# Graph network on one core: the last graph masked and added by VectorE, z stored from ScalarE's queue, the start reordered

## The chip, the cores and the metric

The kernel runs on one core of a Trainium2 chip. Its engines are TensorE (PE: matmuls, with its weight loads as PEld), VectorE (DVE), ScalarE (ACT), GpSimd (POOL) and SyncE (SP), which here only issues DMAs. Each engine runs its own instructions in order; they meet through semaphores. The metric is the device time of one execution in microseconds (us).

## The reference

For each of 16 graphs, x is 512 nodes by 128 features and adj is 512 by 512.

```
h = x                                     # five layers, one GRU cell for all
for l in range(5):
    m   = h @ weight[l]
    agg = (adj != 0)^T @ m
    gi = agg @ w_ih.T + b_ih ;  gh = h @ w_hh.T + b_hh
    r = sigmoid(i_r + h_r); z = sigmoid(i_z + h_z); n = tanh(i_n + r * h_n)
    h = (1 - z) * n + z * h
y = layernorm(x + h * nodemask)
# second network: five groups g of the first 25 nodes, two normalised graph convolutions each
z = layernorm(y + sum_g softmax(fusion_w)[g] * conv(relu(conv(y[idx_g]))))   # rows 0..24; the others get z = layernorm(y)
```

## The kernel before

**The steps.** The 16 graphs times 5 layers are 80 steps k, in an order fixed by the table ROUNDS: graphs 0, 1, 2, 3 in their first layer are steps 0 to 3, then layers of several graphs take turns. State and messages are held transposed, features on the 128 partitions and the 512 nodes along the free axis. Every fp32 operand of a product is split into two fp16 halves (hi and lo), so a product is three matmuls: hi by hi, hi by lo, lo by hi (`split_product`).

**One step.** PE does `aggregate(k)` (8 matmuls over the adjacency held in fp8 as tile A8), `gates_of_state(k)` (9 matmuls of the weights WH by the state into the PSUM banks pHN, pR, pZ) and `gates_of_messages(k)` (9 matmuls of the merged weights WC by the messages AG into pR, pZ, pIN). ACT makes the hi half of the messages (`aggregated_hi`) and the sigmoids and the tanh. DVE makes the lo half (`aggregated_lo`), `candidate(k)` (two operations on tile T) and `new_state(k)` (two operations, the second writes H). POOL makes z*h (`kept_share`, tile ZH) and the lo half of the new state. PE may write pIN of step k only when H of step k-1 is there.

**Loads and transposes.** The adjacency of a graph (1 MB, fp32) is loaded into one of three slots of tile AS and cast to fp8 by DVE in two halves (`cast_half`; graph 0 in four quarters, `cast_first`). In a graph's first layer, its x in natural layout is split by ACT (`natural_hi`) and POOL (`natural_lo`) into tile NAT. From step 2 on, SP issues one DMA transpose per step: in a first layer it turns NAT into the state HT and waits for `natural_lo`; in a later layer it turns HT into NAT, for the aggregation of that step. SP's queue is in order, so a late transpose delays the next. `first_state` (POOL) sums the halves of a new graph's state.

**The start.** PE transposes x of graph 0, w_hh, w_ih and weight[0] (`L834` to `L839`). ACT copies the last two to SBUF (semaphore wi_v) and PE multiplies them (`merge(0, pIN)`), which gives the weights WC of layer 0; ACT and DVE split them (`merged_hi`, `merged_lo`). Then come the state products of step 0 into pHN and pR, the bias rows' transpose and `aggregate(0)` (`first_messages`), then pZ. Nothing here is scheduled by a tool: the order is the order in which the code of each engine is written.

**The end.** The three last steps also carry the tail of the second network: `conv_s` and `conv_d` of PE with copies on ACT between them, and five chained additions `fused` on DVE into tile FU, then the statistics of z (`stats_z`), POOL's power for the inverse root, and `normalise_z` into ZO. For the last graphs, PE transposes H back into PSUM (`back`), the node mask is multiplied on (`masked`, into YM), POOL adds x (`residual`, into Y), DVE makes statistics (`stats`), POOL the inverse roots, DVE the scaled means (`scales`), and ACT and DVE normalise. SP stores each graph in two DMAs (`store_y`, `L387` and `L388`) and z in one (`store_z`, `L393`).

Of the kernel before, what the change touches and what calls it, by code (L numbers as in the profile page):

```python
# [6 lines left out]
ALU = mybir.AluOpType  # L7
# [7 lines left out]
P = 128  # L15
B, N, D = 16, 512, 128
L = 5
NI = N // P
# [7 lines left out]
S = P // Q  # L26
# [88 lines left out]
def graph_net_kernel(nc, x, adj, nodemask, weight, w_ih, w_hh, b_ih, b_hh, W1, b1, W2, b2, fusion_w, out):  # L115
    ctx = ExitStack()
    with ctx:
# [226 lines left out]
        def _(sp):  # L344
# [79 lines left out]
            for b in range(B - 4, B):  # L424
                store_y(b)
            store_z(TAIL)
            for slot in range(4):
# [5 lines left out]
        def _(pool):  # L433
# [192 lines left out]
            normalise(E0, range(2))  # L626
            residual(B - 1)
            inverse_root(B - 2)
# [4 lines left out]
        def _(pe):  # L633
# [39 lines left out]
            def gates_of_state(k, between=lambda: None):  # L673
# [14 lines left out]
                if k > 0:  # L688
                    pe.wait_ge(sig_z, k)
                split_product(pZ, WH[:, 0, 1, :], WH[:, 1, 1, :], ht[0], ht[1], True, False)  # L690

            def gates_of_messages(k, between=lambda: None):
# [83 lines left out]

            def conv_s(groups, bank):
                for j, g in enumerate(groups):
                    for h in range(NH):
                        last = mm(bank[:, j * P:(j + 1) * P], H1[:, h, g, :], W2S[:, g, h, :],  # L780
                                  start=(h == 0), stop=(h == NH - 1))
                last.then_inc(c_mm, 1)

# [41 lines left out]
            def first_messages():  # L825
                pe.wait_ge(ld_r, 16 * 4)
                rows = ROWS.shape[0]
                tr(pC[:, 0:rows], ROWS[:, :], IDF[0:rows, 0:rows]).then_inc(cols_t, 1)
                aggregate(0)

# [8 lines left out]
            tr(pIN[:, 3 * D:4 * D], WL[:, 0, :], IDF[:, :]).then_inc(wi_t, 1)  # L839
            pe.wait_ge(wi_v, 1)  # L840
            merge(0, pIN)
            pe.wait_ge(wh_lo, 1)
            gates_of_state(0, first_messages)
            pe.wait_ge(x_lo, 1)
            transpose_x(1, pF)
# [38 lines left out]
            pe.wait_ge(c_ea, 5 * TAIL + 3)  # L884
            conv_s(range(0, 3), LAST_BANKS[3])
            back(B - 1)
            conv_s(range(3, G), LAST_BANKS[4])
# [6 lines left out]
        def _(act):  # L894
# [155 lines left out]
            natural_hi(1)  # L1050
            load_a(3)
            aggregated_hi(0)
            transposed_hi(1, pF)
            act.wait_ge(cols_v, 1)
            reset_gate(0)
            update_gate(0)
            new_gate(0)
            aggregated_hi(1)
# [45 lines left out]
            normalise(E0, range(2, NI))  # L1104
            masked(B - 1)
            for part, groups in enumerate(LAST_PARTS):
# [5 lines left out]
            normalise(B - 2)  # L1112
            normalise(B - 1, range(2, NI))

        @block.vector
        def _(dve):
# [134 lines left out]
            def normalise(b, blocks):  # L1251
# [4 lines left out]
                last.then_inc(f_dv, 1)  # L1256

            def softmax_shift():
                dve.wait_ge(ld_f, 16)
                link(v.tensor_reduce(FS[:, 1:2], FW[:, :], AX_X, ALU.max))  # L1260
                v.tensor_scalar(FX[:, :], FW[:, :], FS[:, 1:2], None, ALU.subtract).then_inc(fw_x, 1)
# [104 lines left out]
            cast_first(1)  # L1366
            merged_lo(0, pIN)
            cast_first(2)
            cast_first(3)
            dve.wait_ge(cols_t, 1)  # L1370
            link(v.tensor_copy(COLS[:, :], pC[:, 0:COLS.shape[1]]))
# [8 lines left out]
            for k in range(1, K):  # L1380
                if k == 2:
                    cast_half(3, 0)
                new_state(k - 1)
# [18 lines left out]
                for b in range(B):  # L1402
                    if b >= 4 and k == CAST_AT[b] + 1:
                        cast_half(b, 1)
                    if k == FINAL[b] + TURNED[b] + 2 and b < BY_DMA:
                        variances(b)
                candidate(k)
                if k <= 2:
                    aggregated_lo(k + 1)
# [42 lines left out]
            stats(B - 2)  # L1452
            fused(TAIL, range(0, 3))
            stats(B - 1)
            scales(B - 2)
            fused(TAIL, range(3, G))
            stats_z(TAIL)
# [25 lines left out]
```

## Time and profile before

| What | us |
|---|---|
| median of 3 runs | 511.0 (510.79 to 512.11) |
| the profiled execution, whole | 511.83 |
| its span, first to last event | 510.0 |
| PE busy | 492.1 (96%) |
| DVE busy | 382.4 (75%) |
| POOL busy | 311.1 (61%) |
| ACT busy | 300.9 (59%) |

The profiled execution lies 0.83 us above the median, and 1.8 us of its time lie outside its span. PE's granted clock is full (1.00) in every stretch up to 502 us. PE is busy in nearly every slice of the span except the first and the last, so the two ends, some 30 us at the start and some 15 us at the end, are where something else than PE's own work sets the time.

### The profile page before, as it was taken

What the parts mean: (1) busy time and instruction counts of PE and PEld (TensorE: products, weight loads), DVE (VectorE), ACT (ScalarE), POOL (GpSimd) and SP (SyncE); (2) the same over time, 40 slices, a digit from 0 to 9 for tenths busy, and PEclk for the clock granted to TensorE, in tenths of its full rate; (3) what the DMA queues carried; (4) which work ended last, traced back from release to release, by engine and by line L of the source; (5) the groups of instructions that cost most, each with busy time, mean ns of one, the idle gap of its engine ahead of it and who ended that gap; (6) DMA issues with size and microseconds to landing.
All of it is one profiled execution on the core that took longest, in us unless ns stands there. A gap on an engine that the chain in (4) does not pass through costs nothing.

```text
span 510.0 us, 7334 instructions
## 1 busy us (share of the span) xinstructions
PE 492.1 (96%) x2393; PEld 240.3 (47%) x2393; DVE 382.4 (75%) x727; ACT 300.9 (59%) x549; POOL 311.1 (61%) x282
## 2 busy tenths in 40 slices
PE   8999999999999999999999999999999999999992
PEld 5344444444444444444555444445544444564462
DVE  3777876687867788997677889876567878556794
ACT  4546655655656566666656665566565556754564
POOL 3654775757775688775777458766444645424564
PEclk9999999999999999999999999999999999999998
DMA  8768253654626446337826466242143251222212
GB/s 266 231 153 174 48 150 60 185 159 105 134 41 166 107 100 166 83 81 148 195 48 145 123 185 168 61 85 41 22 101 62 59 98 41 62 60 62 59 32 83
DMA packets 131610, 55.45 MB, mean 109 GB/s; under 512 B 95140, under 2 KB 123252, under 8 KB 131572
## 3 DMA queue, kind: packets, MB, share of 16 engines
q1 hardware_dynamic: 106336, 31.93, 30.4%
q10 hardware_dynamic: 25236, 23.05, 14.8%
q8 instruction: 19, 0.31, 0.2%
q14 instruction: 19, 0.16, 0.1%
HBM read 27.70 MB, written 4.19 MB: 63 GB/s over the span
## 4 chain that ended last, share of the span: by engine, by line
PE 77%; DVE 14%; ACT 4%; issue 3%; DMA 1%; ACTq 0%; DVEq 0%
PE pA L664 22%; PE pR L671 5%; PE pR L670 5%; PE pR L669 5%; PE pZ L669 5%; PE pZ L671 5%; PE pZ L670 5%; PE pIN L669 3%; PE pIN L671 3%; PE pIN L670 3%; PE pHN L669 3%; PE pHN L671 3%; PE pHN L670 3%; DVE T L1155 2%; DVE T L1159 2%
## 5 line engine op out<-in xcount | busy, mean ns | idle before, releaser
L484 POOL TENSOR_TENSOR HT<-H,HT 128x512 f16<-128x512 f32 x74 | 89.1, 1204 | 109.5 <-ACT HT L959 109.3
L664 PE MATMUL pA<-A,NAT 128*128 128x512 fp8e4 x640 | 151.2, 379 | 0.2 <-DVE A L1144 0.2
L473 POOL TENSOR_TENSOR ZH<-Z,H 128x512 f32<-128x512 f32 x80 | 102.5, 1281 | 38.7 <-ACT Z L972 37.0
L1155 DVE SCALAR_TENSOR_TENSOR T<-pHN,BHN,R 128x512 f32<-128x512 f32 x80 | 59.9, 748 | 74.8 <-ACT R L965 74.4
L976 ACT ACTIVATE pIN<-T,COLS 128x512 f32<-128x512 f32 x80 | 55.4, 692 | 76.5 <-DVE T L1159 76.4
L664 PEld LDWEIGHTS pA<-A,NAT 128*128 128x128 f16 x640 | 62.5, 98 | 72.1 <-DVE A L1144 0.7
L959 ACT ACTIVATE HT<-H 128x512 f16<-128x512 f32 x74 | 46.7, 631 | 64.3 <-DVE H L1168 64.3
L965 ACT ACTIVATE R<-pR,BRZ 128x512 f32<-128x512 f32 x80 | 54.5, 681 | 26.7 <-PE pR L671 26.5
L1164 DVE SCALAR_TENSOR_TENSOR pIN<-Z,pIN 128x512 f32<-128x512 f32 x80 | 55.1, 689 | 18.8 <-ACT pIN L976 18.7
L1150 DVE TENSOR_TENSOR AG<-pA,AG 128x512 f16<-128x512 f32 x80 | 54.7, 684 | 9.0 <-ACT AG L955 8.8
L955 ACT ACTIVATE AG<-pA 128x512 f16<-128x512 f32 x80 | 47.2, 590 | 20.6 <-PE pA L664 17.8
L1168 DVE TENSOR_TENSOR H<-ZH,pIN 128x512 f32<-128x512 f32 x80 | 54.9, 687 | 3.7 <-POOL ZH L473 1.0
L1159 DVE TENSOR_TENSOR T<-pIN,T 128x512 f32<-128x512 f32 x80 | 55.3, 691 | 3.0 <-PE pIN L671 0.2
L972 ACT ACTIVATE Z<-pZ,BRZ 128x512 f32<-128x512 f32 x80 | 54.7, 684 | 0.0
L669 PE MATMUL pIN<-AG,WC 128*128 128x512 f16 x80 | 30.4, 380 | 3.1 <-DVE H L1168 2.9
L669 PE MATMUL pHN<-HT,WH 128*128 128x512 f16 x80 | 30.4, 380 | 1.1 <-DVE T L1155 0.7
L669 PE MATMUL pR<-AG,WC 128*128 128x512 f16 x80 | 30.3, 379 | 0.8 <-DVE AG L1150 0.8
L670 PE MATMUL pHN<-HT,WH 128*128 128x512 f16 x80 | 30.3, 379 | 0.0
L671 PE MATMUL pHN<-HT,WH 128*128 128x512 f16 x80 | 30.3, 379 | 0.0
L669 PE MATMUL pR<-HT,WH 128*128 128x512 f16 x80 | 30.3, 379 | 0.0
L670 PE MATMUL pR<-HT,WH 128*128 128x512 f16 x80 | 30.3, 379 | 0.0
L671 PE MATMUL pR<-HT,WH 128*128 128x512 f16 x80 | 30.3, 379 | 0.0
(217 smaller groups left out, 845.0 us busy)
## 6 DMA issues: line engine op xcount, KB each, us to landing
AS<-in_adj_dram ACTq DMA_DIRECT2D x13, 1024.0 KB, 6.0
XR<-in_x_dram ACTq DMA_DIRECT2D x16, 256.0 KB, 3.0
XS<-in_x_dram ACTq DMA_DIRECT2D x13, 256.0 KB, 3.2
out_dram<-Y SPq DMA_DIRECT2D x16, 192.0 KB, 2.1
AS<-in_adj_dram SPq DMA_DIRECT2D x2, 1024.0 KB, 10.4
AS<-in_adj_dram SPq DMA_DIRECT2D x4, 256.0 KB, 5.4
NAT<-HT SPq DMA_TRANSPOSE x64, 3.1
XS<-in_x_dram SPq DMA_DIRECT2D x3, 256.0 KB, 8.4
```

The costliest lines, as they stand in the source:

```text
L473: g_.tensor_tensor(ZH[:, :], Z[:, :], H[:, b, :], ALU.mult).then_inc(zh_p, 1)
L484: g_.tensor_tensor(HT[:, b, 1, :], H[:, b, :], HT[:, b, 0, :], ALU.subtract).then_inc(h_lo, 1)
L664: last = mm(pA2[:, k % 2, :], NAT[:, k % 2, h, i, :], A8[:, b, i, :], start=(h == 0 and i == 0), stop=(h == 1 and i == NI - 1))
L669: mm(bank[:, :], w_hi, v_hi, start=start, stop=False)
L670: mm(bank[:, :], w_hi, v_lo, start=False, stop=False)
L671: return mm(bank[:, :], w_lo, v_hi, start=False, stop=stop)
L972: fn(Z[:, :], pZ[:, :], ACT.Sigmoid, bias=BRZ[:, 1:2], scale=UNSCALE).then_inc(sig_z, 1)
L976: fn(pIN[:, :], T[:, :], ACT.Tanh, bias=BI[:, 2:3], scale=UNSCALE).then_inc(n_a, 1)
L1155: v.scalar_tensor_tensor(out=T[:, :], in0=pHN[:, :], scalar=BHN[:, 0:1], in1=R[:, :], op0=ALU.add, op1=ALU.mult).then_inc(t_v, 1)
L1159: v.tensor_tensor(T[:, :], pIN[:, :], T[:, :], ALU.add).then_inc(u_v, 1)
L1164: v.scalar_tensor_tensor(out=pIN[:, :], in0=Z[:, :], scalar=1.0, in1=pIN[:, :], op0=ALU.subtract, op1=ALU.mult).then_inc(e_v, 1)
L1168: v.tensor_tensor(H[:, GRAPH[k], :], ZH[:, :], pIN[:, :], ALU.subtract).then_inc(h_v, 1)
```

## The change

At the start, PE does the first six state products (pHN and pR of step 0) before `merge(0)`, in an order that takes the hi by hi products first, and `merge(0)` moves into `first_messages`, behind the transpose of the bias rows and ahead of `aggregate(0)`. DVE does all four casts of graph 0 before `merged_lo(0)`. ACT issues the load of graph 3's adjacency after `update_gate(0)`, no longer right after `natural_hi(1)`. DVE's first half cast of graph 3 moves from between `aggregated_lo(2)` and `new_state(1)` to behind `candidate(1)`, ahead of `aggregated_lo(2)`.

At the end, the last graph (15) is masked and added by DVE in one operation per block of 128 nodes, read straight from PSUM (`masked_residual`); ACT's `masked(15)` and POOL's `residual(15)` go. PE transposes graph 15 back behind the first group of `conv_s` instead of behind the third. DVE does that graph's statistics and `scales(14)` ahead of all five `fused` additions. The last z is stored by ACT's queue, no longer by SP's.

```diff
 sync:    for b in range(B - 4, B): store_y(b)
-            store_z(TAIL)
 gpsimd:  residual(B - 2); normalise(E0, range(2))
-            residual(B - 1)
 tensor:
+            def first_gates_of_state():
+                hi, lo = HT[:, 0, 0, :], HT[:, 0, 1, :]
+                banks = [(pHN, 2), (pR, 0)]
+                pe.wait_ge(x_hi, 1)
+                pe.wait_ge(wh_hi, 1)
+                for bank, g in banks:
+                    mm(bank[:, :], WH[:, 0, g, :], hi, start=True, stop=False)
+                pe.wait_ge(x_lo, 1)
+                for bank, g in banks:
+                    mm(bank[:, :], WH[:, 0, g, :], lo, start=False, stop=False)
+                pe.wait_ge(wh_lo, 1)
+                for bank, g in banks:
+                    mm(bank[:, :], WH[:, 1, g, :], hi, start=False, stop=(bank is pHN))
+                first_messages()
+                split_product(pZ, WH[:, 0, 1, :], WH[:, 1, 1, :], hi, lo, True, False)
 ...
                 tr(pC[:, 0:rows], ROWS[:, :], IDF[0:rows, 0:rows]).then_inc(cols_t, 1)
+                pe.wait_ge(wi_v, 1)
+                merge(0, pIN)
                 aggregate(0)
 ...
-            pe.wait_ge(wi_v, 1)
-            merge(0, pIN)
-            pe.wait_ge(wh_lo, 1)
-            gates_of_state(0, first_messages)
-            pe.wait_ge(x_lo, 1)
+            first_gates_of_state()
             transpose_x(1, pF)
 ...
-            conv_s(range(0, 3), LAST_BANKS[3])
-            back(B - 1)
+            conv_s(range(0, 3), LAST_BANKS[3], lambda: back(B - 1))   # called after the first group
             conv_s(range(3, G), LAST_BANKS[4])
 scalar:
             natural_hi(1)
-            load_a(3)
 ...
             update_gate(0)
+            load_a(3)
             new_gate(0)
 ...
-            masked(B - 1)
 ...
             normalise(B - 1, range(2, NI))
+            act.wait_ge(z_o, NC)
+            act.dma_start(out[E0:B, 0:S, :], ZO[:, TAIL % 2, :]).then_inc(st_z[TAIL % 2], 16)
 vector:
+            def masked_residual(b):
+                dve.wait_ge(f_mm, b - BY_DMA + 1)
+                dve.wait_ge(st_y[b % 4], 32 * (b // 4))
+                dve.wait_ge(ld_xr[b % 3], 16 * (b // 3 + 1))
+                for i in range(NI):
+                    last = v.scalar_tensor_tensor(out=Y[:, b % 4, i, :], in0=BACK_BANKS[b][:, i * P:(i + 1) * P],
+                                                  scalar=MASK[:, b, i:i + 1], in1=XR[:, b % 3, i, :],
+                                                  op0=ALU.mult, op1=ALU.add)
+                last.then_inc(f_y, 1)
 ...
             cast_first(0)
             cast_first(1)
-            merged_lo(0, pIN)
             cast_first(2)
             cast_first(3)
+            merged_lo(0, pIN)
 ...
-                if k == 2:
-                    cast_half(3, 0)            # ahead of new_state(1)
 ...
                 candidate(k)
+                if k == 1:
+                    cast_half(3, 0)            # ahead of aggregated_lo(2)
 ...
             stats(B - 2)
-            fused(TAIL, range(0, 3))
+            masked_residual(B - 1)
             stats(B - 1)
             scales(B - 2)
+            fused(TAIL, range(0, 3))
             fused(TAIL, range(3, G))
```

PE at the start, before: the merge (into pIN, from tile BD, which holds the weights' scratch) stands ahead of the state products.

```order
L839 MATMUL pIN<-IDF,BD 128x128
L648 MATMUL pIN<-BD 128x384
L669 MATMUL pHN<-HT,WH 128x512
L670 MATMUL pHN<-HT,WH 128x512
L671 MATMUL pHN<-HT,WH 128x512
L669 MATMUL pR<-HT,WH 128x512
L670 MATMUL pR<-HT,WH 128x512
L671 MATMUL pR<-HT,WH 128x512
L828 MATMUL pC<-IDF,ROWS 128x80
L664 MATMUL pA<-A,NAT 128x512 x8
```

PE at the same place now; L697, L700 and L703 are the lines of the new function, L646 is the merge.

```order
L858 MATMUL pIN<-IDF,BD 128x128
L697 MATMUL pHN<-HT,WH 128x512
L697 MATMUL pR<-HT,WH 128x512
L700 MATMUL pHN<-HT,WH 128x512
L700 MATMUL pR<-HT,WH 128x512
L703 MATMUL pHN<-HT,WH 128x512
L703 MATMUL pR<-HT,WH 128x512
L845 MATMUL pC<-IDF,ROWS 128x80
L646 MATMUL pIN<-BD 128x384
L662 MATMUL pA<-A,NAT 128x512 x8
```

The merge went from directly behind the transposes of the weights to directly ahead of the first aggregation, with the six state products and the bias rows' transpose in between.

DVE at the end, before, from `scales` of graphs 12 and 13 on (FU is the sum of z, ST, MV and VE the statistics, NB the scaled means).

```order
L1242 SCALAR_TENSOR_TENSOR NB<-MV,RS 128x4 x2
L1220 BN_STATS ST<-Y 128x6 x4
L1227 BN_AGGR MV<-ST 128x2 x4
L1230 TENSOR_SCALAR VE<-MV 128x4
L1231 TENSOR_SCALAR VE<-MV 128x1
L1336 SCALAR_TENSOR_TENSOR FU<-pR,X 128x128
L1336 SCALAR_TENSOR_TENSOR FU<-pR,FU 128x128 x2
L1220 BN_STATS ST<-Y 128x6 x4
L1227 BN_AGGR MV<-ST 128x2 x4
L1230 TENSOR_SCALAR VE<-MV 128x4
L1231 TENSOR_SCALAR VE<-MV 128x1
L1242 SCALAR_TENSOR_TENSOR NB<-MV,RS 128x4
```

DVE at the same place now; L1278 is the new operation on graph 15.

```order
L1257 SCALAR_TENSOR_TENSOR NB<-MV,RS 128x4 x2
L1235 BN_STATS ST<-Y 128x6 x4
L1242 BN_AGGR MV<-ST 128x2 x4
L1245 TENSOR_SCALAR VE<-MV 128x4
L1246 TENSOR_SCALAR VE<-MV 128x1
L1278 SCALAR_TENSOR_TENSOR Y<-pHN,COLS,XR 128x128 x4
L1235 BN_STATS ST<-Y 128x6 x4
L1242 BN_AGGR MV<-ST 128x2 x4
L1245 TENSOR_SCALAR VE<-MV 128x4
L1246 TENSOR_SCALAR VE<-MV 128x1
L1257 SCALAR_TENSOR_TENSOR NB<-MV,RS 128x4
L1361 SCALAR_TENSOR_TENSOR FU<-pR,X 128x128
```

Four operations came in, and the first three additions into FU went behind graph 15's statistics and graph 14's `scales`.

## Rows read from the trace of the kernel before

**Rows 1.** Page, the chain that ended last, shares of the span by engine.
```profile
PE 77%; DVE 14%; ACT 4%; issue 3%; DMA 1%; ACTq 0%; DVEq 0%
```

**Rows 2.** Waits of PE, 33 to 480 us: total us, times, longest us.
```profile
PE pIN L669 <- DVE H L1168: 2.1, 3, 1.2
PE pHN L669 <- DVE T L1155: 0.7, 1, 0.7
```

**Rows 3.** Timeline of PE at the start: start us, us, engine, line, operation, [idle before].
```profile
7.94 0.91 PE L648 MATMUL pIN<-BD 128*128 128x384 f32 x2 [0.69 <-ACT BD L1048]
8.69 0.38 PE L669 MATMUL pHN<-HT,WH 128*128 128x512 f16 x1
...
10.05 1.89 PE L664 MATMUL pA<-A,NAT 128*128 128x512 fp8e4 x8
...
24.14 0.39 PE L669 MATMUL pHN<-HT,WH 128*128 128x512 f16 x1 [0.29 <-DMA HT<-NAT]
...
28.83 0.39 PE L669 MATMUL pIN<-AG,WC 128*128 128x512 f16 x1 [0.84 <-DVE H L1168]
...
29.49 3.62 PE L664 MATMUL pA<-A,NAT 128*128 128x512 fp8e4 x16
```

**Rows 4.** Timeline of DVE at the start.
```profile
7.58 1.45 DVE L1139 TENSOR_SCALAR A<-AS 128x512 fp8e4<-128x512 f32 x2
...
9.88 0.75 DVE L1139 TENSOR_SCALAR A<-AS 128x512 fp8e4<-128x512 f32 x2
...
25.24 0.69 DVE L1150 TENSOR_TENSOR AG<-pA,AG 128x512 f16<-128x512 f32 x1 [1.27 <-ACT AG L955]
25.85 1.60 DVE L1144 TENSOR_SCALAR A<-AS 128x1024 fp8e4<-128x1024 f32 x1
```

**Rows 5.** Tile A, 0 to 36 us, half casts: ns min/median/max, first and last start.
```profile
L1144 DVE TENSOR_SCALAR A<-AS x6: 684/685/1648, 14.3 to 28.7; 128x1024 fp8e4<-128x1024 f32 x6
```

**Rows 6.** Timelines of ACT's queue and of POOL at the start.
```profile
10.67 0.40 ACTq L926 DMA_DIRECT2D AS<-in_adj_dram  x1
...
15.96 1.71 POOL L473 TENSOR_TENSOR ZH<-Z,H 128x512 f32<-128x512 f32 x1
...
24.63 1.16 POOL L453 TENSOR_TENSOR NAT<-XS,NAT 128x512 f16<-128x512 f32 x1
```

**Rows 7.** Transpose of graph 3 (line L359 near 25.8 us), and its landing after issue.
```profile
L359 SPq DMA_TRANSPOSE HT<-NAT x1: 1233/1233/1233, 25.8 to 25.8; - x1
...
DMA to landing us min/median/max: 3.2/3.2/3.2
```

**Rows 8.** Loads of adjacency 1 (issued 5.75) and 2 (issued 6.99): issue to landing.
```profile
DMA to landing us min/median/max: 8.1/8.1/8.1
...
DMA to landing us min/median/max: 12.6/12.6/12.6
```

**Rows 9.** Timelines of ACT and POOL at the end: graph 15 masked, then added.
```profile
498.36 1.14 ACT L982 ACTIVATE YM<-pHN,COLS 128x128 f32<-128x128 f32 x4 [0.81 <-PE pHN L749]
...
499.58 1.27 POOL L491 TENSOR_TENSOR Y<-YM,XR 128x512 f32<-128x512 f32 x1 [1.25 <-ACT YM L982]
```

**Rows 10.** Timeline of DVE at the end.
```profile
500.90 0.29 DVE L1336 SCALAR_TENSOR_TENSOR FU<-pR,X 128x128 f32<-128x128 f32 x1 [2.67 <-PE pR L786]
...
505.60 0.35 DVE L1359 TENSOR_SCALAR ZO<-FU,MV,RS 128x128 f32<-128x128 f32 x1
```

**Rows 11.** Timeline of DVE: a 128x128 read from PSUM, and four 128x128 statistics.
```profile
484.98 0.35 DVE L1193 SCALAR_TENSOR_TENSOR pA<-pA,ONE,AS 128x128 f32<-128x128 f32 x1
...
496.69 0.87 DVE L1220 BATCH_NORM_STATS2 ST<-Y 128x6 f32<-128x128 f32 x4
```

**Rows 12.** SP's last two issues, and the landing of L388's stores after 505 us.
```profile
506.59 0.44 SPq L388 DMA_DIRECT2D out_dram<-Y  x1
507.08 0.58 SPq L393 DMA_DIRECT2D out_dram<-ZO  x1
...
DMA to landing us min/median/max: 2.1/2.1/2.1
```

More of the change, by code:

```diff
@@ L775, in conv_b, with conv_s @@
                 last.then_inc(c_mm, 1)
-            def conv_s(groups, bank):
+            def conv_s(groups, bank, behind_first=lambda: None):
                 for j, g in enumerate(groups):
@@ L781, in conv_s @@
                                   start=(h == 0), stop=(h == NH - 1))
+                    if j == 0:
+                        behind_first()
                 last.then_inc(c_mm, 1)
```

## The prediction

> **What bounds the kernel now.** I read the page's slices first: PE is at nine tenths in all but the first and the last slice. The chain of waits says the same: 77% of it runs on PE, 14% on DVE [rows 1]. The waits of PE between 33 and 480 us then show how much slack lies in the middle: the two largest come to 2.8 us in 447 [rows 2]. So from about 33 us to the tail PE is never kept waiting, its work isn't changed, and whatever the start wins is carried through whole to the tail; nothing there waits for a clock or a load of its own. That leaves two stretches, and for these the timelines engine by engine.
>
> At the start PE loses time in three places [rows 3]: 0.69 us ahead of the merge, waiting for ACT's copy of the weights; 0.29 us at step 2 for the transpose of graph 2's state; and 0.84 us as a gap, up to 28.83, ahead of pIN of step 2, waiting for H of step 1. At the end PE is done and the rest is a chain over ACT, POOL and DVE: graph 15 is masked on ACT (1.14 us), added on POOL (1.27 us) [rows 9], and meanwhile DVE stands still for 2.67 us until 500.90 [rows 10]. The last stores then leave one behind the other on SP [rows 12].
>
> **Start, first part: the merge.** PE's idle 0.69 us ends at 7.94; it begins at 7.25. The six state products need the split x and the split w_hh. DVE ends the latter just as its casts start, 7.58 [rows 4], and only the fifth and sixth product read that half, so at 0.22 us a product (8.69 to 10.05 are six and the bias rows' transpose [rows 3]) the fifth starts near 8.1: no wait. Six products and the transpose take 1.36 us, so the merge runs from 8.6 for 0.75 us (7.94 to 8.69 [rows 3]), and `aggregate(0)` starts near 9.36 in place of 10.05. Gain 0.69 us. Next late would be graph 0's casts. The last of the four ended at 10.63 [rows 4] because the split of the merged weights stood ahead of two of them; in the new order the four run through, and the aggregation reaches its last quarter only at 9.36 + 1.3 = 10.7. No wait. The split of the merged weights comes later, near 10.7, and is first read by the message products, which start at 12.8. Hidden. If a quarter of the adjacency itself lands late, up to 0.4 us of this gain goes.
>
> **Start, second part: the load of graph 3.** It was issued at 10.67 [rows 6] and now goes out near 15.0, behind `update_gate(0)`. ACT then waits for DVE anyway, so the 0.40 us of issuing costs nothing. It leaves the DMA engines to the loads of graphs 1 and 2, which took 8.1 and 12.6 us from issue to landing [rows 8]. Graph 1's lands at 13.85 in the old order; its first cast would be wanted at 13.7 now and started at 14.3 before [rows 5]. Either way the 0.69 us hold to within 0.15; the bound on the bad side is 0.5, if POOL's next operation gets in ahead of the cast.
>
> **Start, third part: the half cast of graph 3.** Before, it ran from 25.85 for 1.60 us [rows 4], where its shortest takes 0.684 [rows 5], and both operations of `new_state(1)` stood behind it, so that H came just ahead of PE's pIN at 28.83 [rows 3]. Now it runs in DVE's idle 1.27 us ahead of AG of step 2 [rows 4]. H of step 1 comes 1.5 (from the end of AG, 25.93, to the end of the cast, 27.45) and 0.6 to 0.7 us earlier, near 26.7. PE stood idle from 28.83 - 0.84 = 27.99, and since a matmul starts 0.15 before its forerunner's end in the rows (0.38 long, 0.22 apart), it could have gone on at 27.84. It is ready 0.69 earlier, 27.15, and no longer held: pIN starts 28.83 - 27.15 = 1.68 us earlier. That takes in the 0.69, so the cast itself is worth up to 1.0.
>
> It isn't worth all of that. In its new place the cast asks for its turn while POOL works on ZH of step 1. The rows show that a cast beside POOL's work takes 1.60 or 1.65 where it takes 0.68 alone [rows 4, 5], and that POOL's ZH behind such a cast took 1.71 us [rows 6], against 1.27 for the usual one (POOL's addition of the same size, [rows 9]): 0.44 more. The next POOL operation here is graph 3's NAT, which before ran at 24.63 for 1.16 [rows 6], and the transpose of graph 3 was issued as it ended, 25.8, with 1.23 us on SP's queue [rows 7]. SP takes step 4's transpose only behind that, at 27.1 before, and it lands 3.0 to 3.2 us later [rows 7]. With NAT 0.69 earlier but 0.44 held up, step 4's transpose goes out at 26.9 and lands at 30.0. PE gets to that aggregation at 29.49 - 1.68 + 1.73 = 29.5 (16 matmuls in 3.62 - 0.16 us [rows 3], so 1.73 for eight). It waits 0.5 us: a wait in place of the one removed. So the third part gives 1.0 - 0.5 = 0.5.
>
> The Trainium skill ("SBUF — State Buffer", Who interferes with whom) says that DVE in its two-port modes and GpSimd share one port pair as a lock: who comes first holds it for the whole instruction and the other blocks fully. By that rule the held-up NAT is certain if the cast follows ZH directly, and the start gives 1.2; were there no such lock it would give 1.7. The casts above agree with the lock.
>
> Start in all: 0.69 + 0.5 = 1.2 us, between 0.3 (a quarter late, the cast of graph 1 behind POOL, nothing from the third part) and 1.7.
>
> **End: DVE's chain.** ACT's masking and POOL's addition go. `masked_residual` stands on DVE directly behind the statistics of graph 14, at 500.90 - 2.67 = 498.23 [rows 10]. PE's transposes of graph 15, which ended at about 498.3, come four matmuls earlier and are ready a microsecond before. The new operation is not in this trace. From below: four statistics of the same size in a row take 0.87 us [rows 11]. From above: four single reads from PSUM by the same kind of operation at 0.35 [rows 11], 1.4 us. I take 0.97, nearer the row of four in a row, since nothing is waited for between them. DVE's list is otherwise the same, and every other thing that it waits for is early: the first sums, for which DVE waited until 500.90, are now wanted no sooner than that, ACT's copies ahead of them no longer stand behind the masking, and POOL's roots no longer stand behind a 1.27 us addition. So the chain up to ZO shortens by 2.67 - 0.97 - 0.2 (two more semaphore hand-overs) = 1.5 us, between 1.1 and 1.6. ZO starts at 505.60 - 1.5 = 504.1 (start of the span as before), and ACT's two blocks of graph 15, which wait for its scaled means, end 1.5 us earlier as well.
>
> The Trainium skill ("VectorE: DVE Perf Modes", The TRN2 errata) charges a DVE operation that reads PSUM 120 + FD cycles at 0.96 GHz. Estimate by that page: 4 x 248 / 0.96 = 1.03 us, with which the gain would be 0.06 smaller. No row here shows four such operations in a row.
>
> **End: the stores.** Before, graph 15's second store was issued at 506.59 and z's at 507.08 [rows 12]. z now goes out on ACT's queue, beside graph 15's on SP. The last issue is then graph 15's second store, 0.49 us ahead of where z's stood. All three move up by the 1.5. Landing takes 2.1 us [rows 12]; for two queues that send at the same time I charge 0.2. ACT has nothing behind z's wait, so the wait costs nothing. The end gives 1.5 + 0.49 - 0.2 = 1.8 us, between 1.3 and 2.1.
>
> **Sum.** 511.83 - 1.2 - 1.8 = 508.8 for an execution like the profiled one, which lies 0.83 above the median of the runs shown. Off the median: 511.0 - 3.0 = 508.0.
>
> **Rivals.**
> - *Most of the start doesn't come.* Graph 1's cast falls behind POOL's first_state (the loads there were issued while the DMAs were full), and PE meets new waits for transposes at steps 2 to 4, which leave 0.3 of the start; the new operation goes at 0.35 apiece and the stores collide, so the end gives 1.3. For it: two of six casts took 1.6 us in place of 0.69 [rows 4, 5], so the order in which DVE and POOL get in decides. Against it: everything in the stretch moves up together. 511.0 - 1.6 = 509.4.
> - *The middle takes the start's gain back.* PE waits later for transposes or for H because it is early against them. For it: SP's queue and POOL are as long as before. Against it: only 2.8 us of such waits in 447 [rows 2], and these engines' work is released by PE and moves with it. Only the end's lower part stays: 511.0 - 1.3 = 509.7.
> - *The late load of graph 3 blocks DVE.* It is issued 4.3 us later, and the cast that needs it now stands earlier, ahead of AG and H. If it lands after the cast's turn at 23.3, DVE stands with AG of step 2 and H of step 1 behind it, and pIN follows the landing by 2.85 us (cast, AG, two operations of the state). The start breaks even with before at a landing of 28.83 - 2.85 = 26.0, and the whole kernel at 27.8, a time to landing of 12.8 us. The load of graph 2 had 12.6 [rows 8]. For it: that row. Against it: that load was queued behind two others and this one comes when most of theirs has passed, so I estimate a landing near 21. At 16 us to landing, 31.0, the kernel takes 511.0 + 3.2 = 514.2.
> - *The change is nothing at the end,* because the sum of z and not graph 15 sets it: against it stand the 2.67 us of idle DVE. If so, the start's 1.2 alone: 509.8.
>
> **Chances.** The forecast, 508.0 with its own range of 507.3 to 509.0: 0.65. The first rival, 509.0 to 509.5: 0.20. The second and the last together, around 509.7: 0.12. The third: 0.03. A measurement of this kernel can tell 0.3%, 1.5 us, from no change: faster means under 509.5. Faster 0.86, same 0.11, slower 0.03. The range from 507.0 to 509.9 leaves out some of the second rival, the third, and a gain above 4 us.
>
> **What would show it.** Right: no idle PE ahead of the merge, `aggregate(0)` at 9.4; the half cast of graph 3 near 23.3 with 1.1 to 1.2 us; pIN of step 2 near 27.15 without a wait, then a wait of about 0.5 us for a transpose at step 4; from there PE 1.2 us ahead up to the tail; DVE without the 2.67 us, four operations in about 0.97, ZO near 503 on the shifted clock. Wrong: a cast of graph 3 that waits for its load, new waits of PE past 33 us, or DVE idle behind its fifth addition.

## The result, and the profile after

The changed kernel takes 509.17 us in the median (508.3 to 509.96, 9 runs) against 511.0 (510.58 to 512.11, 9 runs). The two medians are 1.8 us apart. The ratio of the runs is 0.9956, with a 95% interval from 0.9943 to 0.9969: 2.2 us less, between 1.6 and 2.9. The sum said 3.0.

The profiled execution took 508.72 us with a span of 506.9, which is 3.1 less than that of before. The two profiled executions therefore differ by more than the kernels do: one lies in the upper half of its runs and the other in the lower. A reader who had only these two would have called the sum exact, and that would have been luck, as the next rows show.

The chain by engine, page of the changed kernel; it now touches POOL and SP, as [rows 1] did not:

```profile
PE 76%; DVE 13%; issue 3%; ACT 3%; DMA 2%; POOL 1%; SPq 0%; ACTq 0%; POOLq 0%; DVEq 0%
```

**Start.** Timeline of PE in the changed kernel (start us, us, operation, idle before); L853 transposes w_hh, L697 is the first state product, L646 the merge, L662 the aggregation:

```profile
5.43 0.55 PE L853 MATMUL pA<-IDF,BD 128*128 128x128 f32 x3
...
6.80 0.38 PE L697 MATMUL pHN<-HT,WH 128*128 128x512 f16 x1 [0.39 <-ACT WH L1059]
...
8.16 0.85 PE L646 MATMUL pIN<-BD 128*128 128x384 f32 x2
...
8.85 1.90 PE L662 MATMUL pA<-A,NAT 128*128 128x512 fp8e4 x8
...
26.72 0.38 PE L667 MATMUL pIN<-AG,WC 128*128 128x512 f16 x1
...
27.37 1.89 PE L662 MATMUL pA<-A,NAT 128*128 128x512 fp8e4 x8
29.68 1.90 PE L662 MATMUL pA<-A,NAT 128*128 128x512 fp8e4 x8 [0.42 <-DMA NAT<-HT]
```

Against [rows 3], PE doesn't wait ahead of the merge, and `aggregate(0)` starts at 8.85, half a microsecond before the 9.36 that the sum had. The reason stands in the first row. In the execution of before, the same three transposes read:

```profile
5.55 0.85 PE L834 MATMUL pA<-IDF,BD 128*128 128x128 f32 x3
```

They lie 0.21 us apart there and about 0.12 here. PE came up to its fast pace earlier in this execution; the spacing differs by nearly the factor between its two levels, 1.2 and 2.4 GHz. The granted clock is 1.00 in both stretches, so that column doesn't show it; the spacing of equal matmuls does. What decides the pace of one execution isn't known; PE's instructions ahead of these transposes are the same. pIN of step 2 starts at 26.72 without a wait, and then comes the forecast wait, 0.42 us, for the transpose of step 4.

Part of the lead is lost again at once. ACT splits graph 1's x ahead of the messages of step 0, and it waits for that x to land:

```profile
10.45 0.63 ACT L954 ACTIVATE NAT<-XS 128x512 f16<-128x512 f32 x1 [0.92 <-DMA XS<-in_x_dram]
10.99 0.58 ACT L969 ACTIVATE AG<-pA 128x512 f16<-128x512 f32 x1
```

So PE stands idle for 0.61 us ahead of the first product of the messages (12.44), where it stood idle for 0.42 before.

DVE and POOL in the same stretch, by their timelines, where `T<-pHN` is the candidate of step 0:

```profile
7.72 1.65 DVE L1154 TENSOR_SCALAR A<-AS 128x512 fp8e4<-128x512 f32 x3 [0.27 <-DMA AS<-in_adj_dram]
9.66 0.43 DVE L1154 TENSOR_SCALAR A<-AS 128x512 fp8e4<-128x512 f32 x1 [0.29 <-DMA AS<-in_adj_dram]
...
13.20 2.26 DVE L1159 TENSOR_SCALAR A<-AS 128x1024 fp8e4<-128x1024 f32 x2
15.38 0.74 DVE L1170 SCALAR_TENSOR_TENSOR T<-pHN,BHN,R 128x512 f32<-128x512 f32 x1
...
22.79 1.34 DVE L1159 TENSOR_SCALAR A<-AS 128x1024 fp8e4<-128x1024 f32 x1
```

```profile
13.34 1.56 POOL L462 TENSOR_TENSOR H<-HT 128x512 f32<-128x512 f16 x1 [1.02 <-DVE HT L1142]
14.86 1.72 POOL L472 TENSOR_TENSOR ZH<-Z,H 128x512 f32<-128x512 f32 x1
...
23.54 1.60 POOL L452 TENSOR_TENSOR NAT<-XS,NAT 128x512 f16<-128x512 f32 x1
```

The last quarter of graph 0's adjacency now keeps DVE waiting (9.66), but PE not yet: its eight matmuls take 1.90 us as before (in four other profiles of the new start with fast transposes a quarter comes too late, and they take 2.00 to 2.17). The half cast of graph 3 takes 1.34 us beside POOL's ZH, and POOL's NAT behind it 1.60 in place of the 1.16 of [rows 6]: the 0.44 us of the sum. The two casts of graph 1 take 2.26 us where two short ones take 1.3. They did so before as well:

```profile
14.30 2.25 DVE L1144 TENSOR_SCALAR A<-AS 128x1024 fp8e4<-128x1024 f32 x2
```

So the change didn't bring this loss, and the sum had no term for it. It turns out to be the largest thing left to win at the start.

**End.** DVE, then SP's and ACT's queues, in the changed kernel's timelines:

```profile
496.54 1.12 DVE L1278 SCALAR_TENSOR_TENSOR Y<-pHN,COLS,XR 128x128 f32<-128x128 f32 x4
...
499.29 0.28 DVE L1361 SCALAR_TENSOR_TENSOR FU<-pR,X 128x128 f32<-128x128 f32 x1
...
502.73 0.35 DVE L1384 TENSOR_SCALAR ZO<-FU,MV,RS 128x128 f32<-128x128 f32 x1 [0.26 <-POOL RS L502]
```

```profile
502.90 0.33 SPq L387 DMA_DIRECT2D out_dram<-Y  x1
503.11 0.61 ACTq L1128 DMA_DIRECT2D out_dram<-ZO  x1
503.27 0.43 SPq L388 DMA_DIRECT2D out_dram<-Y  x1
```

Bytes still flow until 506.1. The changed kernel's stretches (from:to us, length, busy time of each engine, granted clock, DMA share, GB/s):

```profile
504.50:505.00 0.50, 0.00 (x0) 0.00 (x0) 0.00 (x0) 0.00 (x0) 0.00 (x0) 0.50 0.93 237
...
505.75:506.00 0.25, 0.00 (x0) 0.00 (x0) 0.00 (x0) 0.00 (x0) 0.00 (x0) 0.50 0.20 59
506.00:506.25 0.25, 0.00 (x0) 0.00 (x0) 0.00 (x0) 0.00 (x0) 0.00 (x0) 0.50 0.03 8
```

The last bytes come 3.0 us behind z's issue. That the two queues' stores slow each other is likely, since the DMA engines are 0.93 busy there, but no row splits the bytes by store. The 2.67 us of idle DVE in [rows 10] are gone and the four new operations take 1.12. From the start of the last H (494.28) to the end of the span there are 12.62 us, where before there were 14.12 (495.88 to 510.0). The measure has no start of the kernel in it, and it repeats: 14.11 to 14.22 in the four profiles with the old end, 12.51 to 12.70 in the nine with the new one (the kernel whose sums go first apart). So the end is worth 1.4 to 1.7 us in every execution, and what varies is the start.

### The profile page after: what moved, and what is told of

It is laid out like the page before. It is cut to its first block, busy times and chain, and to the rows that moved or that the text cites. A ratio compares the mean times of both kernels' runs of the same rounds, so it can differ in the third digit from the quotient of the medians.

```text
span 506.9 us, 7331 instructions
## 1 busy us (share of the span) xinstructions
PE 491.2 (97%) x2393; PEld 239.7 (47%) x2393; DVE 383.3 (76%) x731; ACT 299.8 (59%) x545; POOL 310.6 (61%) x281
## 4 chain that ended last, share of the span: by engine, by line
PE 76%; DVE 13%; issue 3%; ACT 3%; DMA 2%; POOL 1%; SPq 0%; ACTq 0%; POOLq 0%; DVEq 0%
PE pA L662 22%; PE pZ L669 5%; PE pZ L667 5%; PE pR L669 5%; PE pR L668 5%; PE pZ L668 5%; PE pR L667 5%; PE pIN L667 3%; PE pIN L669 3%; PE pIN L668 3%; PE pHN L667 3%; PE pHN L669 3%; PE pHN L668 3%; DVE T L1170 2%; DVE H L1183 2%
## 5 line engine op out<-in xcount | busy, mean ns | idle before, releaser
L662 PE MATMUL pA<-A,NAT 128*128 128x512 fp8e4 x640 | 151.4, 379 | 0.5 <-DMA NAT<-HT 0.4
L662 PEld LDWEIGHTS pA<-A,NAT 128*128 128x128 f16 x640 | 62.4, 98 | 73.0 <-DMA NAT<-HT 0.9
L667 PE MATMUL pHN<-HT,WH 128*128 128x512 f16 x79 | 30.0, 380 | 1.1 <-DVE T L1170 0.7
L667 PE MATMUL pZ<-HT,WH 128*128 128x512 f16 x80 | 30.3, 379 | 0.0
L668 PE MATMUL pZ<-HT,WH 128*128 128x512 f16 x80 | 30.3, 379 | 0.0
L669 PE MATMUL pZ<-HT,WH 128*128 128x512 f16 x80 | 30.3, 379 | 0.0
L668 PE MATMUL pZ<-AG,WC 128*128 128x512 f16 x80 | 30.3, 379 | 0.0
L669 PE MATMUL pZ<-AG,WC 128*128 128x512 f16 x80 | 30.3, 379 | 0.0
```

The lines of the kernel that those rows point to most:

```text
L662: last = mm(pA2[:, k % 2, :], NAT[:, k % 2, h, i, :], A8[:, b, i, :], start=(h == 0 and i == 0), stop=(h == 1 and i == NI - 1))
L667: mm(bank[:, :], w_hi, v_hi, start=start, stop=False)
L668: mm(bank[:, :], w_hi, v_lo, start=False, stop=False)
L669: return mm(bank[:, :], w_lo, v_hi, start=False, stop=stop)
```

## The experiments

All were timed in five rounds beside the kernel before; each interval is about 0.12%, or 0.6 us, wide on either side. The runs alone therefore can't tell two theories that lie half a microsecond apart. Where that is so the profile decides, by marks: the last H above for the end, and for the start the merge of layer 1, behind which PE has passed every wait of the start.

**The start alone.** The new start with the old end.

> The start of the changed kernel with the end of the kernel before. The measured gain of the whole change is 2.2 us by the ratio, where my sum said 3.0, and the two profiled executions differ by 3.1. Theory A (my sum is right at the start, 1.2 us, and the end falls short): ratio 0.9976, 509.8 us. Theory B (the start is worth 0.6 to 0.8 us, because PE's first transposes run at either of two speeds, 0.21 or 0.11 us apiece, from one execution to the next, and where they run fast the wait ahead of the merge is only partly there to be won; the two profiled executions caught one of each): ratio 0.9987, 510.3. In the profile both expect pIN of step 2 without a wait and one wait of about 0.4 us for a transpose at step 4. B expects aggregate(0) to start at 8.85 when the transposes are fast and 9.36 when they are slow.

Ratio 0.9987 (0.9976 to 0.9998), 0.7 us. The start is worth about half of the 1.2 in my sum, though 1.2 lies just at the edge of the interval. The transposes were fast (0.49 us) and `aggregate(0)` started at 8.85, as theory B had it. What neither theory had is the rest: the profiled execution was the longest of the twelve runs (512.27 us, the others 510.16 to 511.68). PE, DVE and POOL, three timelines:

```profile
15.29 1.02 PE L664 MATMUL pA<-A,NAT 128*128 128x512 fp8e4 x4 [0.69 <-DVE A L1161]
16.87 1.04 PE L664 MATMUL pA<-A,NAT 128*128 128x512 fp8e4 x4 [0.56 <-DVE A L1161]
```

```profile
13.82 3.00 DVE L1161 TENSOR_SCALAR A<-AS 128x1024 fp8e4<-128x1024 f32 x2 [0.52 <-DMA AS<-in_adj_dram]
16.73 0.74 DVE L1172 SCALAR_TENSOR_TENSOR T<-pHN,BHN,R 128x512 f32<-128x512 f32 x1
```

```profile
13.44 1.15 POOL L463 TENSOR_TENSOR H<-HT 128x512 f32<-128x512 f16 x1 [1.06 <-DVE HT L1144]
14.82 1.44 POOL L473 TENSOR_TENSOR ZH<-Z,H 128x512 f32<-128x512 f32 x1 [0.23 <-ACT Z L989]
```

Graph 1's adjacency landed at 13.8 (8.1 us behind its issue, 7.5 in the changed kernel's profile), half a microsecond behind its cast's turn. POOL's sum had started at 13.44. The first cast waited for it, the second for ZH, and the candidate of step 0 started at 16.73 where the changed kernel's has 15.38. That is 1.35 us, and PE stands still for it: 0.6 because the casts start later, 0.74 because they take 3.00 in place of 2.26. How often this happens isn't shown. It is the only one of the six profiles with the new start, the early load and no wait of POOL in which the load lands behind the casts' turn; of the twelve runs, four lie 0.7 us or more above the other eight.

**The end alone.** The new end with the old start.

> The end of the changed kernel with the start of the kernel before. From H of step 79 (end) to the end of the span the kernel before has 13.45 us and the changed one 11.93 us, 1.5 less. Theory A (the end falls short in the runs): under 1.2 us, ratio above 0.9977. Theory B (the end is what the profile says): 1.5 us, ratio 0.9971, 509.5 us. If the start and the end add up, e1 and e2 together give 2.2.

Ratio 0.9967 (0.9955 to 0.9979), 1.7 us; 12.61 us from the last H to the end, against 14.12. With the 0.7 of the start that makes 2.4 against 2.2 measured together. The runs only just leave out the theory that the end falls short (under 1.2 us); the mark bears out the other, 1.5. This execution shows the old start with the fast transposes:

```profile
5.34 0.49 PE L851 MATMUL pA<-IDF,BD 128*128 128x128 f32 x3
...
7.06 0.91 PE L646 MATMUL pIN<-BD 128*128 128x384 f32 x2 [0.79 <-ACT BD L1064]
...
9.18 1.89 PE L662 MATMUL pA<-A,NAT 128*128 128x512 fp8e4 x8
```

Its aggregation starts at 9.18; the new start with fast transposes has 8.85. So at this pace the new order is worth some 0.33 us here and not 0.69. The transposes themselves don't start at the same time in every execution. Counted from their start, the aggregation comes after 3.84 and 3.86 us in the two old orders with fast transposes and after 3.37 to 3.42 in six new ones; the first product of the messages comes after 7.23 and 7.25 against 6.91 to 7.11. So 0.46 us reach the aggregation and some 0.2 the messages, for landings hold up the rest.

The mark of the start, the merge of layer 1, tells the pace from the change. First the old start, with slow transposes (the kernel before) and with fast ones (this kernel):

```profile
34.88 0.81 PE L648 MATMUL pF<-BD 128*128 128x384 f32 x2
34.01 0.81 PE L646 MATMUL pF<-BD 128*128 128x384 f32 x2
```

Then the new start, slow (the kernel with the sums first, below) and fast (the changed kernel):

```profile
33.63 0.81 PE L646 MATMUL pF<-BD 128*128 128x384 f32 x2
33.36 0.81 PE L646 MATMUL pF<-BD 128*128 128x384 f32 x2
```

Slow against slow, the start is worth 1.25 us, all that the sum had. Fast against fast it is worth 0.65. In the execution with the late load the mark is at 34.66, which is 0.65 worse than the old start. The two profiled executions of the result are slow before and fast after. They differ by 1.52 at this mark, and that made up for what the end lacked.

**The cast of graph 3 alone.**

```diff
-                if k == 2:
-                    cast_half(3, 0)
+                if k == 1:                     # behind candidate(1)
+                    cast_half(3, 0)
```

> The kernel before, with the first half cast of graph 3 alone moved behind candidate(1). By my step: pIN of step 2 starts 1.0 us earlier, then PE waits about 0.4 for the transpose of step 4, which POOL's held-up NAT makes late; net 0.6 us, ratio 0.9988. The rival that the lock between DVE and POOL plays no part: 1.0 us, ratio 0.998, and POOL's NAT operation of graph 3 takes its usual 1.16 us where mine expects 1.60. A rival that the early half cast blocks DVE on its load: AG of step 2 later than before and no gain.

Ratio 0.9998 (0.9987 to 1.0008): inconclusive in the runs, since the 0.6 us expected lies inside the interval. Its profile shows each step of mine, with the POOL operation held up:

```profile
23.84 1.61 POOL L453 TENSOR_TENSOR NAT<-XS,NAT 128x512 f16<-128x512 f32 x1
```

The merge of layer 1 starts at 33.61 here and at 34.01 in the end-only kernel, which has the same old start and also fast transposes: 0.40 us.

**The merge and the first casts alone.**

```diff
-            pe.wait_ge(wi_v, 1); merge(0, pIN); pe.wait_ge(wh_lo, 1)
-            gates_of_state(0, first_messages)
+            first_gates_of_state()             # merge(0) inside first_messages
```

> The kernel before, with the merge behind the state products and the four casts of graph 0 ahead of merged_lo, and nothing else. By my step: aggregate(0) starts 0.69 us earlier and all that follows moves with it, ratio 0.9986. Rival (B): with fast transposes the last quarter of graph 0's adjacency and the landing of graph 1's x hold up PE and ACT, and only 0.3 to 0.4 us come: ratio 0.9993. The profile shows which of the two speeds it caught by the time of the transposes of w_hh (x3: 0.85 or 0.55 us).

Ratio 0.9991 (0.9981 to 1.0001), 0.5 us, in the middle of the two forecasts; the interval holds both, and no change too. The profile caught the slow transposes, and there the step is as I had worked it out:

```profile
5.60 0.85 PE L855 MATMUL pA<-IDF,BD 128*128 128x128 f32 x3
...
9.37 1.89 PE L664 MATMUL pA<-A,NAT 128*128 128x512 fp8e4 x8
```

9.37 against 10.05 in [rows 3], 0.68 us, and the same mark is at 34.19 against 34.88. So the merge's new place gives 0.69 us when PE comes up to pace late, and less when it comes early.

**z on SP's queue.**

```diff
+            store_z(TAIL)                      # sync, behind store_y(15)
-            act.wait_ge(z_o, NC)
-            act.dma_start(out[E0:B, 0:S, :], ZO[:, TAIL % 2, :]).then_inc(st_z[TAIL % 2], 16)
```

> The changed kernel with z stored on SP's queue again, behind graph 15's stores. In the changed kernel's trace z is issued on ACT's queue at 503.11, among graph 15's stores on SP's (502.90 and 503.27), and DMA data flows until 506.1, 3.0 us behind z's issue, where z alone at the end of the queue took 2.1 before. Theory A (my step: the second queue is worth 0.3 us): this kernel ends 0.3 later than the changed one behind H of step 79, 12.9 us. Theory B (what the queue saves in issuing is lost in landing, since both stores share the DMA engines): 12.6 us, the same within 0.1. In the runs both lie within 0.1% of the changed kernel: ratio 0.996.

Ratio 0.9955; 12.51 us from the last H to the end, against 12.62. This is its theory B: the second queue gives nothing, though here z is issued last, and later:

```profile
503.30 0.43 SPq L388 DMA_DIRECT2D out_dram<-Y  x1
503.77 0.58 SPq L393 DMA_DIRECT2D out_dram<-ZO  x1
```

**Graph 3's NAT ahead of ZH of step 1 on POOL.**

```diff
-            kept_share(1)
             natural_lo(3)
+            kept_share(1)
```

> The changed kernel with POOL's natural_lo(3) ahead of kept_share(1), so that graph 3's NAT is ready before the half cast of graph 3 holds POOL up. If the wait of PE at step 4 comes from the chain NAT of graph 3, transpose of graph 3, transpose of step 4 on SP, as my step had it: that transpose is issued near 25.3 in place of 26.5 and PE's wait of 0.42 us goes; 0.4 us faster than the changed kernel, ratio to before 0.9948. If the transpose of step 4 waited for something else, the wait stays and the ratio is 0.9956.

Ratio 0.9949 (0.9935 to 0.9962). The 0.4 us against the changed kernel's 0.9956 are inside the intervals, but the wait is gone, as the two aggregations in one row show:

```profile
27.50 3.62 PE L662 MATMUL pA<-A,NAT 128*128 128x512 fp8e4 x16
```

**The load of graph 3 back in its old place.**

```diff
             natural_hi(1)
+            load_a(3)
 ...
             update_gate(0)
-            load_a(3)
```

> The changed kernel with the load of graph 3's adjacency back where it was, issued near 10.7. Theory C: whether graph 1's adjacency lands before or behind its cast's turn decides a further 1.3 us at step 1. In the profile of the start alone it landed at 13.8 with the cast's turn at 13.3; POOL's first_state(1) came in first and the two casts took 3.0 us together, where the changed kernel's profile (landed 13.2) has 2.26. With graph 3's load sharing the DMA engines from 12 us on, graph 1's lands later, 8.1 us or more behind its issue, and the late case is the usual one: 0.4 to 0.8 us slower than the changed kernel, ratio 0.997 to 0.9972. If the place of that load doesn't matter: 0.9956.

Ratio 0.9961 (0.9948 to 0.9974). Theory C was wrong in this part: graph 1's adjacency landed 7.3 us behind its issue with the old place as well, and no difference can be told from the changed kernel. The move of that load is worth nothing that shows here.

**POOL yields to the casts.**

```diff
+            pool.wait_ge(a_cast, 2)
             first_state(1)
             kept_share(0)
```

> The changed kernel with one more wait: POOL's first_state(1) waits for both half casts of graph 1, so that the casts are never held up by POOL. Theory C: the casts take 0.68 us each, the candidate of step 0 starts by 15.4 whether the load lands at 13.2 or 13.8, and POOL's sum and ZH behind them still end before H of step 0 needs ZH. The late case goes: on average 0.3 to 0.7 us faster than the changed kernel, ratio 0.9942 to 0.995, and a smaller spread of the runs. If the lock plays no part in the spread: 0.9956, and an unchanged spread of 1.7 us.

Ratio 0.9935 (0.9923 to 0.9948), 1.1 us better than the changed kernel, though the two intervals just touch: more than I expected. The two casts now read

```profile
13.20 1.29 DVE L1160 TENSOR_SCALAR A<-AS 128x1024 fp8e4<-128x1024 f32 x2
14.41 0.74 DVE L1171 SCALAR_TENSOR_TENSOR T<-pHN,BHN,R 128x512 f32<-128x512 f32 x1
```

With the load in time, the second cast had been held up in the changed kernel too (2.26 us for the pair): the wait saves 0.97 us in the good case. The mark moves by as much, from 33.36 to 32.38. Four of the five runs lie within 0.4 us, and one is some 1.3 above them; that one is not explained.

**A late load of graph 1, without and with that wait.**

```diff
             load_x(1)
+            load_x(2)
             load_a(1)
-            load_x(2)
```

> The changed kernel with SP's load of graph 2's x ahead of that of graph 1's adjacency, so that the latter is issued and lands some 0.6 us later, near 13.8. Theory C (the late landing lets POOL's first_state(1) in ahead of the casts, and each of the two casts then waits for a POOL operation): the two casts take 3.0 us together in place of 2.26, the candidate of step 0 starts near 16.7 in place of 15.4, and the kernel is 1.0 to 1.3 us slower than the changed one: ratio 0.998. The rival that a late landing costs only its own lateness: 0.5 us, ratio 0.9966.

> The same late load, with POOL's first_state(1) waiting for the casts. Theory C: each cast takes 0.68 us from the landing on, the candidate of step 0 starts 1.4 us behind the landing, near 15.3, and the kernel takes 0.5 us more than with that wait and the early load: ratio 0.9944, 1.8 us faster than the late load without the wait. If POOL's operations are not what prolongs the casts, the wait changes nothing: ratio as with the late load alone.

Without the wait: 0.9974 (0.9963 to 0.9984), 0.9 us slower than the changed kernel. With it: 0.9949 (0.9936 to 0.9962), 1.3 us faster than without. The DVE timelines, first without, then with the wait:

```profile
14.36 2.37 DVE L1159 TENSOR_SCALAR A<-AS 128x1024 fp8e4<-128x1024 f32 x2 [1.34 <-DMA AS<-in_adj_dram]
16.64 0.74 DVE L1170 SCALAR_TENSOR_TENSOR T<-pHN,BHN,R 128x512 f32<-128x512 f32 x1
```

```profile
14.50 1.30 DVE L1160 TENSOR_SCALAR A<-AS 128x1024 fp8e4<-128x1024 f32 x2 [1.52 <-DMA AS<-in_adj_dram]
15.71 0.75 DVE L1171 SCALAR_TENSOR_TENSOR T<-pHN,BHN,R 128x512 f32<-128x512 f32 x1
```

The candidate starts where expected (16.7) without the wait, though by a path that I hadn't foreseen: the load was so late that POOL's sum was over, and only the second cast was held up, by ZH. With the wait it starts 1.2 us behind the first cast, at 15.7 in place of the 15.3 expected, since the load itself landed only at 14.5. So POOL getting in costs about 1 us beyond the lateness of the load. But it costs as much when the load is early (0.97), and the lateness by itself costs 0.7 to 0.9 us, with the wait and without. The part of theory C that is about late loads, that both casts are then held up (3.0 us), did not happen here (2.37); it stands on the one profile of the start alone. That profile without the wait is also the slowest of its eight runs (511.02).

**Sums first.** The changed kernel with three `fused` additions ahead of `masked_residual`.

```diff
+            fused(TAIL, range(0, 3))
             masked_residual(B - 1)
 ...
-            fused(TAIL, range(0, 3))
```

> The changed kernel with DVE's first three fused additions ahead of masked_residual again. My step at the end was that masked_residual and graph 15's statistics pay because they fill the time in which DVE waited for the sums. The sums in pR are there near 498.3 on the clock of the changed kernel's profile, DVE is free at 496.5: with the additions first it stands idle for 1.7 us, and all behind it is 1.7 later. From H of step 79 to the end 14.3 us in place of 12.6, ratio 0.9989: then taking ACT's and POOL's operations out gives nothing by itself and the order gives the whole 1.5. The rival that shortening the path of graph 15 is what counts: under 13.4 us, ratio below 0.9972.

Ratio 0.9997 (0.9988 to 1.0006), and 14.77 us from the last H to the end, 0.5 more than expected: the whole gain of the end is gone, and 0.65 us besides.

```profile
498.67 0.29 DVE L1361 SCALAR_TENSOR_TENSOR FU<-pR,X 128x128 f32<-128x128 f32 x1 [1.69 <-PE pR L803]
```

DVE waits 1.69 us for the sums, and what follows is later by that and more. Taking the masking off ACT and the addition off POOL gives nothing by itself; what pays is that this work fills the time in which DVE waited for the sums.

**Both repairs.** The wait of POOL for the casts, and graph 3's NAT ahead of ZH of step 1.

> The changed kernel with both repairs: POOL's first_state(1) waits for the casts of graph 1 (worth 1.1 us in the runs), and natural_lo(3) stands ahead of kept_share(1) (0.3 us alone). In the profile of the first repair alone PE no longer waits at step 4 either, so the second has nothing left to win: same as the first alone, ratio 0.9935, 508.2 us. If the two add up: 0.9928.

507.75 us in the median, five runs from 507.57 to 507.89, ratio 0.9923 (0.9909 to 0.9936): 3.9 us better than the kernel before, 1.7 better than the changed one. It is the best version measured. The interval overlaps that of the first repair alone, so that the second adds something is not shown, though four of these five runs lie below all five of those.

## Why the prediction came out as it did

The direction, the place of both gains and the range from 507.0 to 509.9 were right; the size was 3.0 for 2.2. The measured 509.17 lies outside the forecast's own band (507.3 to 509.0) and in that of the first rival (509.0 to 509.5, chance 0.20). In part that rival's mechanism is what happened: less of the start, and in one profile graph 1's cast behind POOL. But it left too little: 0.3 of the start, where the runs of the start alone have 0.7, and 1.3 of the end, where the marks have 1.5.

- *The middle carries the gain through.* Right. Between the mark at 33 to 35 us and the last H there are 460.9 to 461.1 us in the profile of before, of the change and of ten others. Two are longer, the start alone (461.7) and the late load without the wait (462.0), each with one more wait of PE for a transpose, between 100 and 200 us (0.6 and 0.9). They are the two in which the candidate of step 0 starts last (16.73 and 16.64; 16.47 before); how that leads to the wait stays open.
- *The merge, 0.69 us.* This is the term of the start that was mis-sized. It is exact where PE's transposes run slowly, as in the one trace that I had. Where they run fast, which eight of the fourteen profiles show, ACT's split of w_hh and the landings of graph 0's last quarter and of graph 1's x hold the chain, and 0.2 to 0.46 are left. By the marks the whole start then gives 0.65 in place of 1.2. I took the pace of one execution for that of all.
- *The casts of graph 1, "either way the 0.69 us hold to within 0.15; the bound on the bad side is 0.5".* The bound failed: in one profile of the start alone the load landed behind the cast's turn, POOL got in ahead of both casts, and the loss was 1.35 us. It was named as a rival's mechanism, with too low a price: the operation that gets in costs its own time, and then the next one does it again. How much of the missing 0.5 us is due to this and how much to the pace isn't shown. An old start with fast transposes has the cast's turn at 13.43, hardly later than the new one (13.20), so part of this risk is the pace's and not the change's.
- *The cast of graph 3 and the new wait.* Right in each part: pIN 0.43 earlier than written on a start that was half a microsecond early, cast 1.34, NAT held up by 0.44, the wait at step 4 0.42 for 0.5. The Trainium skill ("SBUF — State Buffer", Who interferes with whom) has one port pair as a lock for the whole instruction; the rows agree a second time, and the kernel in which POOL yields shows by intervention that the two hold each other up.
- *DVE's chain at the end, 1.5 us.* Measured 1.27 (ZO behind the last H: 9.72 before, 8.45 after). The four operations took 1.12 for 0.97, 0.34 each and 0.26 apart. With 1.12 the sum gives 1.35; the rest, 0.08, goes into a wait that it didn't have, of ZO for POOL's root (0.26 us idle). PE's transposes of graph 15 come eight matmuls earlier, not four, and were in time. My value was nearer the statistics than the PSUM reads, and the truth lay between. The estimate by the Trainium skill ("VectorE: DVE Perf Modes", The TRN2 errata), 1.03 us, was closer to the 1.12, though low as well.
- *The stores, 0.3 us.* Before, z was ready at 505.95 but stood behind graph 15's stores in the queue until 507.08 [rows 12], so the end hung on those stores and not on ZO. Counted from the last H, graph 15's second store is issued 1.72 us earlier (10.71 before, 8.99 after), and the last issue of all 2.21 earlier, 1.72 and the 0.49. But the span ends 3.63 us behind that last issue, where it ended 2.92 behind it: the second queue, for which I charged 0.2 without a row to go by, cost 0.7. That is the mis-sized term of the end. With z on SP's queue the three stores move by 1.6 to 1.7 and the end is no later. With 1.50 for 1.8 the end is the smaller part of the error, 0.3 of the 0.8; the start has the other 0.5.
- The rivals on the slower side, the late load of graph 3 above all, did not occur: it landed 7.0 us behind its issue, at 20.9, and the cast wanted it at 22.8.

## What to carry to other kernels

Before a start is made earlier, look at what its operations will meet: the landing of a load that was comfortably ahead can become the last to arrive. Where DVE's and POOL's operations hold each other up on the path, fix their order with a wait (here one line was worth half as much as the whole change); the row that called for it, two casts in 2.25 us, stood in the trace of before. Profile a start more than once, and compare stretches between marks that don't contain it: two profiles alone would have confirmed a sum that was a third too high.

## What the runs showed of the hardware

- PE's first fp32 transposes lie 0.21 or 0.11 us apart from one execution to the next, with a granted clock of 1.00 in both: 0.85 and 0.49 us for three. With the old start this moves the whole kernel's mark by 0.87 us (34.88 and 34.01).
- A half cast (128 x 1024, fp32 to fp8) takes 0.68 us alone and up to 1.65 beside POOL; POOL's operations are held up by 0.3 to 0.45 us in turn. With POOL waiting, each cast is 0.68 again.
- Four reads from PSUM by one operation each, 128 x 128, masked and added, take 1.12 us in a row.
- Two stores issued within 0.4 us on two queues landed no sooner than one behind the other on one queue: 12.62 and 12.51 us from the last H to the end.
